# q, k and v projected from fp16 halves in three products, and the expert weights bounded by sums of squares on ScalarE

## What is computed

```
h = layernorm(x) * (1 + ca) + sa
q = relu(h Wq' + bq);  k = relu(h Wk' + bk);  v = h Wv' + bv
for each token t:   s = gamma*s + k_t v_t';  z = gamma*z + k_t
                    y_t = (q_t s) / (q_t . z + 1e-6)
x = x + ga * y
h = layernorm(x) * (1 + cb) + sb
e = argmax(h Wr' + br)                       # one expert of 8 for each token
x = x + gb * (relu(h W1[e]' + b1[e]) W2[e]' + b2[e])
```

## Time and profile before

| | |
|---|---|
| time, median of 3 (lowest, highest) | 466.65 us (466.51, 466.78) |
| profiled execution's own time | 469.77 us |
| its span | 467.5 us |
| TensorE matmul busy | 439.2 us (94%) |
| VectorE busy | 385.9 us (83%) |
| ScalarE busy | 305.1 us (65%) |
| GpSimd busy | 260.2 us (56%) |
| mean granted TensorE clock | 0.977 |

### The profile page before, as it was taken

How to read it: one execution, slowest core, us unless ns; L and a number is a source line. 1 busy time by engine, 2 the same in 40 slices (tenths; PEclk the granted TensorE clock), 3 DMA queues, 4 the chain that set the end, 5 groups by cost and what they waited for, 6 DMA issues and landing times.

```text
span 467.5 us, 13656 instructions
## 1 busy us (share of the span) xinstructions
PE 439.2 (94%) x4296; PEld 392.0 (84%) x4296; DVE 385.9 (83%) x1012; ACT 305.1 (65%) x804; POOL 260.2 (56%) x429
## 2 busy tenths in 40 slices
PE   7999999999999999995767999999999999999992
PEld 4898889999889988893436999989999999999991
DVE  2548999999999999999985887787887777888862
ACT  1335666666666666664606877878777888778870
POOL 2112577777667766756346465656656556664332
PEclk9999999999999999997779999999999999999997
DMA  8725344444444444411015243443333443442110
GB/s 281 254 81 175 119 159 158 158 158 153 152 147 153 156 157 147 136 47 68 25 32 141 59 104 76 110 100 88 87 85 90 87 116 78 97 58 57 45 29 2
DMA packets 43572, 51.71 MB, mean 111 GB/s; under 512 B 24811, under 2 KB 37356, under 8 KB 41328
## 3 DMA queue, kind: packets, MB, share of 16 engines
q1 hardware_dynamic: 37552, 36.67, 27.1%
q0 software_dynamic: 4992, 12.60, 9.8%
q10 hardware_dynamic: 960, 1.57, 1.0%
HBM read 35.22 MB, written 13.50 MB: 104 GB/s over the span
## 4 chain that ended last, share of the span: by engine, by line
PE 76%; DVE 13%; issue 3%; DMA 3%; DVEq 2%; ACT 1%; POOL 1%; ACTq 0%; POOLq 0%
PE ps_o L1434 17%; PE ps_qk L1351 11%; PE ps_qk L1420 9%; PE ps_va L1420 9%; PE ps_va L1361 6%; PE ps_o L1310 5%; PE ps_kv L1317 5%; PE ps_va L1338 3%; PE ps_o L1306 3%; DVE w L1123 2%; DMA w<-in_wmod 2%; DVE arena L1109 2%; PE ps_k L1189 2%; DVEq L1127 1%; PE ps_x L1231 1%
## 5 line engine op out<-in xcount | busy, mean ns | idle before, releaser
L1434 PE MATMUL ps_o<-w,arena 128*128 x936 | 108.7, 273 | 0.6 <-DVE arena L1109 0.4
L1434 PEld LDWEIGHTS ps_o<-w,arena 128*128 128x128 f16 x936 | 89.8, 98 | 10.9 <-issue 1.2
L1123 DVE COPY w<-w 128x2048 f16 x78 | 59.2, 760 | 34.5 <-PE ps_va L1420 23.9
L660 ACT ACTIVATE arena<-ps_qk,arena 128x128 f32<-128x128 f32 x156 | 44.6, 368 | 41.9 <-PE ps_qk L1420 39.1
L1351 PE MATMUL ps_qk<-arena,wqk_b 128*128 128x128 f32 x512 | 62.4, 275 | 0.0
L1420 PE MATMUL ps_qk<-arena,w 128*128 128x128 f16 x936 | 58.7, 219 | 3.6 <-DVE w L1123 1.9
L544 POOL DMA_INDIRECT out_rows<-arena,slot_token x39 | 42.1, 1081 | 34.5 <-POOL arena L540 30.6
L1351 PEld LDWEIGHTS ps_qk<-arena,wqk_b 128*128 128x128 f32 x512 | 59.7, 192 | 0.0
L1420 PEld LDWEIGHTS ps_qk<-arena,w 128*128 128x128 f16 x936 | 55.2, 98 | 5.3 <-issue 2.4
L1420 PE MATMUL ps_va<-arena,w 128*128 128x128 f16 x936 | 58.6, 219 | 0.2 <-DVE w L1123 0.2
L1109 DVE TENSOR_TENSOR arena<-arena 128x512 f16<-128x512 f32 x78 | 53.3, 683 | 4.7 <-ACT arena L668 3.7
(11 more groups left out here) (192 smaller groups left out, 834.2 us busy)
## 6 DMA issues: line engine op xcount, KB each, us to landing
w<-in_w_raw SPq DMA_DIRECT2D x16, 1024.0 KB, 5.1
token_rows<-arena SPq DMA_DIRECT2D x64, 128.0 KB, 1.9
arena<-in_x SPq DMA_DIRECT2D x32, 128.0 KB, 2.1
b_sb<-in_b2b SPq DMA_DIRECT2D x1, 1024.0 KB, 5.3
w<-in_wmod ACTq DMA_DIRECT2D x1, 768.0 KB, 8.7
w<-in_wqkv SPq DMA_DIRECT2D x1, 768.0 KB, 8.1
arena<-token_rows,slot_token POOLq DMA_INDIRECT x39, 3.6
out_rows<-arena,slot_token POOLq DMA_INDIRECT x39
```

What stands on the lines that cost most here:

```text
L660: last = act.activation(hid[:, f, :], bank[("qk", "va")[h]][:, (f % 4) * P:(f % 4 + 1) * P], ACT.Relu, bias=consts_now[:, r, f:f + 1], sca ...
L1123: dve.tensor_copy(now[:, :, i * F // 2:(i + 1) * F // 2], of[:, :, i * F // 2:(i + 1) * F // 2]).then_inc(s_w1, 1)
L1434: last = pe.matmul(bank[f"o{n % 2}"][:, 0:D], hid_parts[:, r % 2, b, f, :], w[:, bass.ds(m, 1), a, f * D:(f + 1) * D].rearrange("p a d -> ...
```

## The change

The two expressions in the title are two changes in one. **Projections:** h and the q, k and v weights are scaled by powers of two and split into two fp16 halves each. q, k and v are then three products of halves (`PARTS`), as the experts' already are. The scales come from bounds taken in the head; the biases, the decay, the denominator's constant and the column of ones carry them. ScalarE writes the high half of h, VectorE the low one (`h_lo`, at its slot's end), and TensorE waits for the second. **Bound:** `max_piece` goes. ScalarE squares and sums half a matrix (1024 columns) at the end of each slot (`square_half`, L580 of the changed kernel), and TensorE waits for two of those per pair where it waited for `max_piece`. `HID_SCALE` and the floors change values only.

```diff
-HID_SCALE = 2.0 ** -23
+HID_SCALE = 2.0 ** -20
+HALVES = 2
+X_ONE = 2.0 ** 10
+PARTS = ((0, 0), (0, 1), (1, 0))
@@ ScalarE @@
+            def square_half(k, u):
+
+                if (m := matrix_at(k, MAX)) is not None:
+                    if u == 0:
+                        act.wait_ge(s_wraw, 16 * (m + 1))
+                    need(act, s_wboth, HALVES * m + u)
+                    half = raw_w[:, landing(m), u * (MW // HALVES):(u + 1) * (MW // HALVES)]
+                    act.activation(squares, half.rearrange("p (b c) -> p b c", b=B), ACT.Square,
+                                   accum_out=w_piece[:, m, u:u + 1]).then_inc(s_wboth, 1)
...
-                    act.activation(h_t[:, r], bank["x"][:, 0:D].rearrange("p (k t) -> p k t", k=DK),
-                                   ACT.Copy).then_inc(s_ht, 1)
+                    act.activation(h_t[:, r, 0], bank["x"][:, 0:D].rearrange("p (k t) -> p k t", k=DK),
+                                   ACT.Copy, scale=X_ONE).then_inc(s_hhs, 1)
...
-                    act.wait_ge(s_modt_ready, 1)
+                    act.wait_ge(s_ss, 1)
                     for h in range(DK):
-                        last = act.activation(wqk_b[:, u, :, h, :], wqkv_sb[:, 0:2, h, :], ACT.Copy,
-                                              scale=scale_at[:, h, u:u + 1])
-                    last.then_inc(s_wqk, 1)
+                        last = act.activation(wqk_b[:, u, 0, :, h, :], wqkv_sb[:, 0:2, h, :], ACT.Copy,
+                                              scale=scale_qk[:, h, u:u + 1])
+                    last.then_inc(s_whq, 1)
+                if (k, u) == (-1, 1):
+                    act.wait_ge(s_sv, 1)
+                    for b in range(B):
+                        act.activation(wv_b[:, b, 0], wv_f[:, b], ACT.Copy, scale=v_scale).then_inc(s_whv, 1)
                 hi_piece(k, u, 1)
+                square_half(k, u)
@@ VectorE @@
+            def power_of_two(largest, scale, whole, back):
+
+                step(dve.tensor_scalar(head_bits.bitcast(I32), largest.bitcast(I32), EXPONENT, None, ALU.bitwise_and))
+                step(dve.tensor_scalar(scale.bitcast(I32), head_bits.bitcast(I32), -1.0, float((TOP + 254) * EXP_ONE),
+                                       ALU.mult, ALU.add))
+                dve.tensor_scalar(back.bitcast(I32), head_bits.bitcast(I32), float(-(TOP + 10) * EXP_ONE), None, ALU.add)
+                step(dve.tensor_scalar(whole, scale, X_ONE, None, ALU.mult))
...
+            def qk_lo(b):
+                dve.wait_ge(s_whq, b + 1)
+                for h in range(DK):
+                    last = dve.scalar_tensor_tensor(wqk_b[:, b, 1, :, h, :], wqkv_sb[:, 0:2, h, :],
+                                                    scale_qk[:, h, b:b + 1], wqk_b[:, b, 0, :, h, :], ALU.mult,
+                                                    ALU.subtract)
+                last.then_inc(s_wqk, 1)
...
+            def h_lo(k, u):
+                if it := att_item(k, u, XPOSE):
+                    n, g, r = it
+                    dve.wait_ge(s_hhs, n + 1)
+                    dve.scalar_tensor_tensor(h_t[:, r, 1], bank["x"][:, 0:D].rearrange("p (k t) -> p k t", k=DK),
+                                             X_ONE, h_t[:, r, 0], ALU.mult, ALU.subtract).then_inc(s_ht, 1)
...
+                step(dve.tensor_reduce(v_most[:, 0:1], wv_f.rearrange("p b h c -> p (b h c)"), AX_X, ALU.max,
+                                       apply_absolute_value=True))
+                dve.memset(scales[:, 14:15], 0.0).then_inc(s_wvm, 1)
...
-            def max_piece(k, u, j):
-                if (m := matrix_at(k, MAX)) is None:
-                    return
-                i = 2 * u + j
-                if i == 0:
-                    dve.wait_ge(s_wraw, 16 * (m + 1))
-                last = dve.tensor_reduce(w_piece[:, m, i:i + 1], raw_piece(m, i), AX_X, ALU.max,
-                                         apply_absolute_value=True)
-                if i == PIECES - 1:
-                    last.then_inc(s_wboth, 1)
             def lo_piece(k, u, j, last=False):
...
+                    qk_bound()
                     router_scale()
+                    qk_scales()
+                    router_centre()
                     v_weights(0)
-                    router_centre()
                     v_weights(1)
+                    h_lo(-1, 1)
+                    qk_lo(0)
+                    router_columns()
                     projection_biases()
+                    v_scales()
+                    v_lo(0)
+                    qk_lo(1)
+                    v_lo(1)
                     b1_bound()
                 first_stats(k, u)
...
-                        dve.tensor_reduce(w_most, bank["va"][:, W_AT:W_AT + PIECES + 1], AX_X, ALU.max).then_inc(s_wmax, 1)
+                        dve.tensor_reduce(w_most, bank["va"][:, W_AT:W_AT + HALVES + 1], AX_X, ALU.add).then_inc(s_wmax, 1)
...
+                h_lo(k, u)
...
-                max_piece(k, u, 1)
@@ TensorE @@
-                        pe.wait_ge(s_wboth, m + 1)
+                        pe.wait_ge(s_wboth, HALVES * (m + 1))
                         if m == 1:
                             pe.wait_ge(s_floor, 1)
-                        pe.matmul(bank["va"][:, W_AT:W_AT + PIECES + 1], con("ones"), w_piece[:, m, :], start=True,
+                        pe.matmul(bank["va"][:, W_AT:W_AT + HALVES + 1], con("ones"), w_piece[:, m, :], start=True,
                                   stop=True)
                     for h in range(DK):
...
+                    if n == 0:
+                        pe.wait_ge(s_wvm, 1)
+                        pe.matmul(bank["o0"][:, 0:1], con("ones"), v_most[:, 0:1], start=True, stop=True).then_inc(s_wvs, 1)
                     for m in range(2):
                         for c in range(DK):
-                            for h in range(DK):
-                                last = pe.matmul(bank["qk"][:, (m * DK + c) * P:(m * DK + c + 1) * P],
-                                                 wqk_b[:, r, m, h, c * P:(c + 1) * P], h_t[:, r, h, :],
-                                                 start=(h == 0), stop=(h == DK - 1))
+                            for q, (a, b) in enumerate(PARTS):
+                                for h in range(DK):
+                                    last = pe.matmul(bank["qk"][:, (m * DK + c) * P:(m * DK + c + 1) * P],
+                                                     wqk_b[:, r, a, m, h, c * P:(c + 1) * P], h_t[:, r, b, h, :],
+                                                     start=(q == 0 and h == 0), stop=(q == 2 and h == DK - 1))
                     last.then_inc(s_qkp, 1)
-                    if n == 0:
-                        router_through_v()
-                        pe.wait_ge(s_wvb, 1)
+                    need(pe, s_wvb, min(n + 1, B))
                     need(pe, s_att, n)
                     need(pe, s_xe, n)
-                    for h in range(DK):
-                        last = pe.matmul(bank["va"][:, 0:DV], h_t[:, r, h, :], wv_b[:, r, h, :],
-                                         start=(h == 0), stop=(h == DK - 1))
+                    for q, (a, b) in enumerate(PARTS):
+                        for h in range(DK):
+                            last = pe.matmul(bank["va"][:, 0:DV], h_t[:, r, b, h, :], wv_b[:, r, a, h, :],
+                                             start=(q == 0 and h == 0), stop=(q == 2 and h == DK - 1))
                     last.then_inc(s_vp, 1)```

The first place is ScalarE at the end of a slot of the attention stage and the start of the next (`mod_rows_sb` is where the squares go that nobody reads, `w_piece` the sums; `ps_x` is the transposed x, `ps_k` the transposed k, `rs` the deviations). Before:

```order
L570 ACTIVATE w<-w,w_scale 128x512
L616 ACTIVATE arena<-ps_x 128x256 [waits v_projected,x_transposed]
L623 ACTIVATE arena<-arena,rs 128x256 [waits x_transposed,rstd1]
L570 ACTIVATE w<-w,w_scale 128x512
L580 ACTIVATE arena<-ps_k,decay 128x256 [waits kv_done,k_transposed]
L592 ACTIVATE arena<-arena,rs 128x256 [waits h2_ready,rstd2]
L603 ACTIVATE arena<-ps_qk,bqk_t 128x128 [waits qg_ready,scores_done,qk_projected]
```

More of the change, by code:

```diff
@@ L254, in build @@
         filler = sb("filler", [P, 512], F16)
+        scales = sb("scales", [P, 16])
+        qk_most, v_most = scales[:, 0:2], scales[:, 2:4]
+        qk_sum, qk_scale, qk_all, qk_back = (scales[:, i:i + 1] for i in range(4, 8))
+        v_sum, v_scale, v_all, v_back = (scales[:, i:i + 1] for i in range(8, 12))
+        den_eps, head_bits = scales[:, 12:13], scales[:, 13:14]
+        scale_qk = sb("scale_qk", [P, DK, B])
+        squares = gate_b.bitcast(F16)
         c16 = sb("c16", [P, 3 * P + NT + NCH], F16)
@@ L774, in router_scale, with qk_bound @@
                 dve.wait_ge(s_u, 1)
+            def qk_bound():
+                dve.wait_ge(s_wqkv, 32)
+                dve.tensor_reduce(qk_most[:, 0:1], wqkv_sb[:, 0:2].rearrange("p m h d -> p (m h d)"), AX_X, ALU.max,
```

(38 more changed lines are left out.)

69 lines of the change are left out of this document (43 added, 26 removed).

## The result

| | before | changed |
|---|---|---|
| median of 4 runs, us | 466.71 | 473.91 |
| profiled execution, own time, us | 469.77 | 472.97 |
| its span, us | 467.5 | 471.0 |

The changed kernel is slower: the ratio is 1.0134, 95% interval 1.0083 to 1.0184. Forecast were 472.9 us, a range of 464.5 to 477.5 and slower with 75%.

A forecast was written before the change was run, and what follows sets the result against it. The loop in which ScalarE and GpSimd wait for each other was to bound the pair at 12.25 us. Terms +3.4, -2.2, +3.6, +1.0 and +0.4 sum to +6.2 us: median 466.65 becomes 472.9, range 464.5 to 477.5.

The forecast's parts named there:

- head: Before chunk 1: small instructions ahead of the v weights and VectorE's work behind them start the projection 3.4 us later.
- last pair: End of the steady loop: 12.25 us and 0.4 more, the high half waiting for VectorE, against 11.66 before: +1.0 us.
- chunk 1 to 5: First two pairs: one without weight pieces at 10.57 us and one at 11.70, against 24.50 before: -2.2 us.
- twelve pairs: Steady part, chunk 5 to chunk 29: 12.25 us a pair for 11.95, +3.6 us.
- to the last bound's product: Stage's end, from last projection to last scores: 5.52 us before, with longer VectorE and ScalarE steps now, +0.4 us.
- Path 2: Loop of ScalarE and GpSimd waiting for each other, lengthened by the square: 12.25 us a pair, said to decide.
- blocked turns: GpSimd instructions held up behind VectorE's over shared ports: 0.88 us of the ScalarE-GpSimd loop, said to stay.
- Path 1: TensorE waiting for ScalarE's square ahead of the scores in the u = 1 slot: 11.70 us a pair.
- first rival: GpSimd not blocked: its loop falls under 11.70 us a pair, the squares' wait decides, time 465.9 us; 20%.
- small rival of 84 ns: TensorE's fp16 products slow among fp32 ones, 84 ns each, a slot 0.68 us longer, time some 486; 3%.

The follow-up runs named there:

- experiment 1: Changed kernel with GpSimd making the second norm's deviations ahead of the first norm's: pair 11.74 us, ratio to before 1.009.
- 2: Changed kernel with TensorE's product of the squares' sums behind q and k of the same slot, except slot 16: pair 11.79 us, ratio to before 1.0078.
- Experiment 7: Changed kernel with the squares of slots 14 and 15 ahead of ScalarE's high pieces: last pair 11.91 us for 15.23, ratio to before 1.004.
- two edits: Changed kernel with second norm's deviations first on GpSimd and the bound's product behind q and k; both together: pair 10.76 us, ratio to before 0.978.

## Why the prediction was right, and where its sum was off

The sign held, and half of the mechanism: two engines lost work and the steady pair did not follow, since ScalarE's square lengthened two paths. Only the forecast had the paths make each pair 0.30 us longer, and it became 0.06 shorter; pairs of 12.1 to 12.4 were to show the forecast right, and they are 11.89. What made the kernel slower is the last pair, and the head, whose 2.5 us use up the 2.3 that the first two pairs gain. Term by term, from the profiled executions:

| term | predicted, us | measured, us |
|---|---|---|
| head, chunk 1 later by | 3.4 | 2.5 |
| chunk 1 to 5 | -2.2 | -2.3 |
| twelve pairs | +3.6 (12.25 each) | -0.7 (11.89 each) |
| last pair | +1.0 | +3.6 |
| to the last bound's product | +0.4 | +0.6 |
| sum there | +6.2 | +3.7 |

- **Head.** What stands behind the v weights came out to the digit, in sum: 3.65 us were expected, the weights ended at 17.85 and the projection started at 21.50. Too much were the 0.7 us for the small instructions ahead of the weights, which went beside TensorE's setup. (The prediction's own terms give 22.29 less 18.82, 3.5 and not 3.4 us.) No experiment took the head's delay away.
- **Path 2.** ScalarE's part is 5.50 (5.49 predicted), with the square's step 1.04 (1.0). GpSimd's part is 6.48 here and 6.32 one pair before, not 6.76: a loop of 11.8 to 12.0, not 12.25. The step that failed is that I took out q's wait alone and kept the rest of the earlier trace rows: with that wait go also the 0.29 us of "issue" ahead of the deviations and 0.1 of the step to qg, since GpSimd now works end to end. The blocked turns stayed, one L459 of 1.25 for 0.71 and one qg of 1.23 for 0.73, together 1.0 where I had 0.88. The Trainium skill, SBUF — State Buffer, Terms, shared port pair, says that VectorE and GpSimd lock each other out of one pair of ports: the trace agrees, each long one stands behind VectorE's L955 (the L459 of 142.38 behind one of 142.34), and four fewer L869 a pair freed none.
- **Path 1.** 11.70 predicted, 11.74 in experiment 1. That the loop is the longer of the two is shown by 1 and 2 together, though by some 0.1 us and not by 0.55: alone the loop takes 11.79, or 11.84 without its first pair, and path 1 takes 11.74. The changed kernel's 11.89 is a little more than either. So the first rival, with pairs of 11.70 and a time of 465.9, was nearer in the pair than the forecast; it missed by the last pair, which it had at +0.6.
- **Last pair.** The term that was most mis-sized: I gave 0.4 us for the high piece that waits for VectorE; it is 1.91 us of wait on ScalarE and 3.04 on TensorE, and then a lower clock, some 1.2 us more on q and k alone. Experiment 7 took 3.3 us of it away. I had seen the wait and did not ask where VectorE's low piece itself would stand.
- **The errors cancelled.** -4.3 on the pairs, -0.9 in the head and +2.6 on the last pair leave +3.7 for +6.2 at the end of the stage. Routing began 4.7 later and the spans differ by 3.5; where the 1.2 us between came back is open. A second pair of errors cancelled in the step from the profile to the median. The prediction put the profiled execution at 476.0 us and took off 3.1, the distance to the median that the kernel before has; it was 472.97 us, 3.0 less, and stands 0.9 below its median, not 3.1 above. That the median hit 472.9 so closely is therefore luck. The fall of the clock in the head was in none of my cases, but it doesn't explain the 7.2 us between the medians: without the execution of 480.42 us the median is 473.4.
- **fp16 products** between fp32 ones cost the same as in their own stream; q and k, then v on TensorE's timeline:

```profile
132.45 1.50 PE L1446 MATMUL ps_qk<-arena,wqk_b 128*128 128x128 f16 x24
133.79 0.86 PE L1455 MATMUL ps_va<-arena 128*128 128x272 f16 x6
```

1.34 us from start to start, 56 ns each, as taken from the earlier trace rows. The small rival of 84 ns is out.

## What to carry to other kernels

Work that moves from a full engine to a half-empty one is not free if that engine stands in a loop with a third: add the loop up, all the way round. When two paths come out within a few per cent of each other, removing either shows almost nothing, so judge such edits together: here two edits that showed 0.4 to 0.6% each, hardly clear of noise, turned a loss of 1.3% into a gain of 2.2%. Look separately at the first and the last pass of a pipeline, where waits exist that the steady part hasn't.

## What the runs showed of the hardware that was not expected

A sum beside an activation is an instruction of its own, 0.19 to 0.24 us long but only about 0.1 us from start to start (L580 above). And the granted clock can fall in one execution and not in another of the same kernel, at the same place, after the same hole of 1.9 us in TensorE's work (at about 20 us, in the head), to 0.50 for 12 us and at a price of 5.3 us.
